# Early products of the first layer: two matmuls of 256 columns into one sum, in place of one of 512 columns

## The chip, the cores and the metric

The kernel runs on one NeuronCore of a Trainium2 chip. The time is what the device takes for one execution, in microseconds. The kernel before took 904.02 us in the median of three runs (903.44 to 906.75).

## The reference

A graph of 3125 nodes with 256 features and 103125 edges, sorted by destination. `x` is normalised and passed through a relu, then three graph convolutions follow, are added to `x`, are normalised again, and one message-passing step with a GRU cell ends it. Cut to what matters:

```python
deg = segment_sum(ones, dst) ; dinv = rsqrt(deg)          # self-loops included
def conv(h, W, b):                                        # three times
    h = h @ W
    return segment_sum(h[src] * (dinv[src] * dinv[dst]), dst) + b
h = relu(layernorm(x))
x = x + conv(relu(conv(relu(conv(h, W1, b1)), W2, b2)), W3, b3)
h = relu(layernorm(x))
red = segment_sum(h[src] + relvectors[edge_type], dst)
x = x + gru_cell(red, h)
```

The kernel replaces gather and segment sum by products with a dense matrix of edge counts, `count` (source nodes by destination nodes, small integers in f16). The factors `dinv` go to the rows of the table before the product and to the rows of the sum behind it. So that f16 suffices, each table of node rows is held as two f16 parts: a high part, and a low part with what the high one leaves over.

## The kernel before

Nodes lie in T = 25 tiles of 128 (the last has 53). `count` is `[128, 25, CW]`: tile of sources, then column of the destination. `node_a` and `node_b` are `[128, 25, 2, 256]`: tile, part (0 high, 1 low), feature.

**Building `count`** (`build_pe`, `build_dve`, `build_act`, `build_sp`, lines 797 to 1232). The edges go through in NS = 202 steps of 512. For each step VectorE writes one-hot rows (`one_hot`, line 927; for two steps at a time, into three sets of buffers), TensorE makes four matmuls of 175 columns (line 815) into a window of 20 destinations in one of four PSUM banks, with one of 25 columns (line 826) for edges that pass into the next window, and ScalarE copies the window into `count` (line 1127). Each fourth step has four matmuls of 80 columns for the relations (line 855). The columns of three of the four matmuls are computed by register instructions of TensorE's sequencer (`span_of`). TensorE waits for the one-hot rows and for the copy of the window three steps before; VectorE waits until TensorE is through with the set of buffers.

**The first layer beside it.** From step 18 on the table of the first layer is ready in `node_a`. Since the edges are sorted, whole columns of `count` are final early, and the first layer's sums for destination tiles 0 to 20 (`EARLY = 21`) are made while `count` is still being built: 21 x 25 = 525 matmuls (`early_product_pe`, line 909), laid between the matmuls of the windows by a fixed schedule (`products_after`, line 753), two or three in a step. The stationary operand is `count[:, t, u * P:u * P + m]`, the moving one the 512 columns of both parts of `node_a` tile `t`; the sums of tile `u` take a whole PSUM bank, one of three (`out_slot`): 256 columns from the high part, 256 from the low. After the last window the tiles 21 to 24 follow in the same manner (line 1287, 100 matmuls).

**Behind each tile.** VectorE takes the sums (`out_bias_dve`, line 1088): line 1094 scales the low half and adds the bias into `scaled`, line 1097 scales the high half and adds `scaled` into `work` and frees the bank. ScalarE applies relu and factor (line 1105) and writes the high part (line 1109), VectorE the low part (line 1114), and SyncE stores the tile to DRAM (line 1187), from which it is read back into `node_b` after the last window. In the order of its instructions VectorE reaches line 1094 about 5 steps after the tile's last product, and line 1114 about 12 steps after it.

**Afterwards** the second and third layer and the message step use `sums_pe` (line 1258: table stationary, `count` moving, 512 columns and a last chunk of 53), `conv_pe` (line 1269, f32) and the GRU (lines 590 to 685, f32).

Of the kernel before, what the change touches and what calls it, by code (L numbers as in the profile page):

```python
# [5 lines left out]
ALU = mybir.AluOpType  # L6
# [5 lines left out]
P = 128  # L12
# [13 lines left out]
REL_BANK, OUT_BANK = 4, 5  # L26
# [4 lines left out]
OUT_SLOTS = 3  # L31
# [20 lines left out]
def program(nc, x, src, dst, rel, convs, relvec, w_ih_t, w_hh_t, b_ih, b_hh, x1_dram, table_dram, out):  # L52
    N, D = x.shape
    E = src.shape[0]
    R = relvec.shape[0]
    T = -(-N // P)
# [19 lines left out]
    SP, PE, DVE, ACTE, POOL = nc.sync, nc.tensor, nc.vector, nc.scalar, nc.gpsimd  # L76

    def rows(t):
        return P if t < T - 1 else TAIL

    with ExitStack() as ctx:
        def sb(name, shape, dt):
            return ctx.enter_context(nc.sbuf_tensor(name, shape, dt))

        def sem(name):
            return ctx.enter_context(nc.semaphore(name))


        count = sb("count", [P, T, CW], F16)
        node_a = sb("node_a", [P, T, 2, D], F16)  # L90
# [5 lines left out]
        work = [sb(f"work{i}", [P, D], F32) for i in range(2)]  # L96
        scaled = [sb(f"scaled{i}", [P, D], F32) for i in range(2)]
        xt = [sb(f"xt{i}", [P, D], F32) for i in range(2)]
# [9 lines left out]
        newt = sb("newt", [P, 4, T], F32)  # L108
# [6 lines left out]
        ps = ctx.enter_context(nc.psum_tensor("ps", [P, 8, BANK], F32))  # L115
# [137 lines left out]
        dve_seq, act_seq = Count(sem("dve_seq")), Count(sem("act_seq"))  # L253
# [72 lines left out]
        def settled(u):  # L326

            return SETTLE_FIRST + SETTLE_STEP * (u // 2) + SETTLE_ODD * (u % 2)
# [427 lines left out]
        summed_at = [next(s for s in range(NS) if products_after[s] >= (u + 1) * T) for u in range(EARLY)]  # L756

        def out_slot(u):

            return ps[:, OUT_BANK + u % OUT_SLOTS, :]  # L760

        def turned_x(t):
            return h1[:, t, :].rearrange("p (f n) -> p f n", f=HALVES)
# [33 lines left out]
        def build_pe():  # L797
            PE.wait_ge(keys_out, 5)
            offset_words.extend(load_offsets(1))
            for s in range(NS):  # L800
# [42 lines left out]
                for u, t in due[len(between):]:  # L843
                    early_product_pe(u, t)

        def between_pe(products, j):
            for u, t in products[len(products) * j // (QUARTERS - 1):len(products) * (j + 1) // (QUARTERS - 1)]:
                early_product_pe(u, t)
# [60 lines left out]
        def early_product_pe(u, t):  # L909
            m = rows(u)  # L910
            if t == 0:
                PE.wait_ge(win_written, settled(u))
                PE.wait_ge(tile_looped, u + 1)
                if u >= OUT_SLOTS:
                    PE.wait_ge(conv_read, u - OUT_SLOTS + 1)
                else:
                    PE.wait_ge(table_ready, T)
            last = PE.matmul(out_slot(u)[0:m, :], count[:, t, u * P:u * P + m], node_a[:, t, :, :].rearrange("p a d -> p (a d)"),  # L918
                             start=(t == 0), stop=(t == T - 1), skip_group_check=True)
            if t == T - 1:  # L920
                last.then_inc(conv_done, 1)

# [18 lines left out]
        def build_dve():  # L941
# [26 lines left out]
            for u in range(EARLY):  # L968
                if summed_at[u] + OUT_AT >= NS:
                    out_bias_dve(u)  # L970
                if summed_at[u] + OUT_LOW_AT >= NS:
                    out_low_dve(u)
# [115 lines left out]
        def out_bias_dve(u):  # L1088
            m, k = rows(u), u % 2
            DVE.wait_ge(conv_done, u + 1)  # L1090
            DVE.wait_ge(bias1_in, 16)
            if u >= 2:
                DVE.wait_ge(node_scaled, u - 1)
            DVE.scalar_tensor_tensor(out=scaled[k][0:m, :], in0=out_slot(u)[0:m, D:2 * D], scalar=newt[0:m, 1, u:u + 1], in1=xt[1][0:m, :],
                                     op0=ALU.mult, op1=ALU.add).then_inc(*dve_seq.up())
            DVE.wait_ge(*dve_seq.now)
            DVE.scalar_tensor_tensor(out=work[k][0:m, :], in0=out_slot(u)[0:m, 0:D], scalar=newt[0:m, 1, u:u + 1], in1=scaled[k][0:m, :],
                                     op0=ALU.mult, op1=ALU.add).then_inc(conv_read, 1)

        def out_shape_act(u):  # L1100
# [143 lines left out]
        def sums_pe(h, nodes, c, f, tail_rows, ready_at, between):  # L1244

            cols = min(CHUNK, N - c * CHUNK)
            b, read = sums_bank(h)
            if read:
                PE.wait_ge(sums_out, read)
            first = ready_at is not None  # L1250
            sources = [t for t in order if t != T - 1] if first else range(T - 1)

            for n, t in enumerate([T - 1, *sources] if h % 2 and tail_rows == TAIL else [*sources, T - 1]):
                k = P if t < T - 1 else tail_rows
                if first:
                    PE.wait_ge(*ready_at(t))
                for part in range(2):
                    last = PE.matmul(ps[:, b, 0:cols], nodes[0:k, t, part, f * P:(f + 1) * P],  # L1258
                                     count[0:k, t, c * CHUNK:c * CHUNK + cols],
                                     start=(n == 0 and part == 0), stop=(n == T - 1 and part == 1))  # L1260
                if n == T - 1:
                    last.then_inc(sums_done, 1)
                between(n)
# [15 lines left out]
        def layers_pe():  # L1279

            PE.wait_ge(win_written, NS)
            PE.wait_ge(chunk_looped, 1)
            for u in range(EARLY, T):
                m = rows(u)
                PE.wait_ge(conv_read, u - OUT_SLOTS + 1)
                for t in range(T):
                    last = PE.matmul(out_slot(u)[0:m, :], count[:, t, u * P:u * P + m], node_a[:, t, :, :].rearrange("p a d -> p (a d)"),  # L1287
                                     start=(t == 0), stop=(t == T - 1))
                last.then_inc(conv_done, 1)

            for layer, nodes in ((1, node_b), (2, node_a)):
                h0 = (layer - 1) * H_LAYER
                for i, c in enumerate(chunks):
                    for f in range(HALVES):
                        ready_at = None if i or f else first_ready if layer == 1 else (lambda t: (node_ready, T + place[t] + 1))
                        sums_pe(h0 + HALVES * i + f, nodes, c, f, TAIL, ready_at, nothing)
                        if f == 0 and i:
                            convs_pe(layer, h0, i - 1)
                convs_pe(layer, h0, NC - 1)

            h0 = 2 * H_LAYER
            PE.wait_ge(chunk_looped, 2)
            PE.wait_ge(rel_placed, NS)
            due = []
            for i, c in enumerate(chunks):
                for f in range(HALVES):
                    def between(n):
                        if n == T // 2 and due:
                            gru_pe(h0, due.pop(0))
                    sums_pe(h0 + HALVES * i + f, node_b, c, f, REL_ROW + R, (lambda t: (node_ready, 2 * T + place[t] + 1)) if i == 0 and f == 0 else None, between)  # L1310
                    if due:
                        gru_pe(h0, due.pop(0))
                assert not due
                due = [place[t] for t in tiles_of[c]]
            for n in due:
                gru_pe(h0, n)

        def convs_pe(layer, h0, i):
            c = chunks[i]
            PE.wait_ge(sums_out, h0 + HALVES * (i + 1))  # L1320
            PE.wait_ge(w_in[layer], 16)
            for t in tiles_of[c]:
                conv_pe(layer * T + place[t], layer, t, t * P - c * CHUNK, agg)
# [3 lines left out]
        def gru_pe(h0, n):  # L1327
            t = order[n]
            i = chunks.index(t * P // CHUNK)
            at_col = t * P - chunks[i] * CHUNK  # L1330
            PE.wait_ge(sums_out, h0 + HALVES * (i + 1))
            gru_tile_pe(order, n, [gru_sums[i % 2][f][:, at_col:at_col + rows(t)] for f in range(HALVES)])
# [222 lines left out]
        with nc.If(verdict_reg == 0):  # L1555
            build_pe()
            layers_pe()
            build_dve()
            layers_dve()
            build_act()  # L1560
            layers_act()
            build_sp()
            layers_sp()
            fast_pool()
# [174 lines left out]
        with nc.Else():  # L1739
            for t in range(T):  # L1740
# [7 lines left out]
                                     op0=ALU.mult, op1=ALU.mult).then_inc(*dve_seq.up())  # L1748
# [92 lines left out]
```

## Time and profile before

| | |
|---|---|
| median of three runs | 904.02 us (903.44 to 906.75) |
| the profiled execution, whole | 906.02 us |
| its span in the profile | 902.1 us |
| granted TensorE clock, mean over the span | 0.988 |
| build of `count` with early products | 97 to 288 us of the span |
| products of tiles 21 to 24 | 288.6 to 310.4 us |

The page gives for each engine its busy time; a matmul's recorded length contains the time in which it runs out of the array, so that lengths of neighbours overlap, and the distance from one start to the next is what a matmul costs TensorE. Idle time is counted only where nothing recorded runs, so waits shorter than that overlap are seen in the starts alone. `x4` in a row of the timeline means four instructions merged: the length reaches from the first one's start to the last one's end.

### The profile page before, as it was taken

To read this page: it belongs to the slowest core of one execution; us is meant where nothing else is said; L and a number is where in the kernel's file an instruction comes from. 1 tells how busy PE (TensorE), PEld (TensorE's weight loads), DVE (VectorE), ACT (ScalarE), POOL (GpSimd) and SP (SyncE) were. 2 spreads that over 40 slices of the span, in tenths; PEclk is the share of its full clock that TensorE was granted. 3 is DMA by queue.
4 is the path that set the end of the run, shared out by engine and by line. 5 is a ranking of instruction groups with operands and counts; after the bars stand their busy time and mean duration, and the time that the engine had idled before them with its cause. 6 is when DMAs were issued, how large, how long until landed. Compare 5 with 4: busy or idle time off the path is not lost.

```text
span 902.1 us, 14157 instructions
## 1 busy us (share of the span) xinstructions
PE 862.2 (96%) x4870; PEld 480.5 (53%) x4870; DVE 451.5 (50%) x1139; ACT 290.3 (32%) x609; POOL 82.0 (9%) x244
## 2 busy tenths in 40 slices
PE   2689999999999999999999999999999999999996
PEld 1348666666666454444455444445464555555554
DVE  6966899999996211221041433227162233333336
ACT  3365667667675100110020201222231112222122
POOL 0210300111000055540000000000000000000000
PEclk9989999999999999999999999999999999999999
DMA  6100000000001400000000101112310000000001
GB/s 197 31 2 1 3 17 22 17 16 23 16 23 50 137 3 3 3 2 1 1 0 30 47 23 41 38 39 70 123 33 20 12 24 24 24 24 24 24 26 42
DMA packets 36998, 28.34 MB, mean 31 GB/s; under 512 B 12869, under 2 KB 35553, under 8 KB 36924
## 3 DMA queue, kind: packets, MB, share of 16 engines
q1 hardware_dynamic: 36252, 26.97, 9.9%
q8 instruction: 43, 0.70, 0.3%
q10 hardware_dynamic: 672, 0.41, 0.2%
q14 instruction: 31, 0.25, 0.1%
HBM read 17.56 MB, written 9.81 MB: 30 GB/s over the span
## 4 chain that ended last, share of the span: by engine, by line
PE 92%; DVE 4%; ACT 1%; issue 1%; SPq 0%; DMA 0%; DVEq 0%
PE ps L1258 43%; PE ps L918 13%; PE ps L815 8%; PE ps L1269 5%; PE ps L640 5%; PE ps L643 5%; PE ps L1287 2%; PE ps L648 2%; PE ps L651 2%; PE ps L899 2%; PE ps L867 1%; DVE node_b L927 1%; PE ps L855 1%; PE ps L887 1%; PE ps L627 1%
## 5 line engine op out<-in xcount | busy, mean ns | idle before, releaser
L1258 PE MATMUL ps<-count,node_b 128*128 128x512 f16 (+3 forms) x1400 | 270.5, 351 | 0.4 <-DVE node_b L1419 0.3
L1258 PEld LDWEIGHTS ps<-count,node_b 128*128 128x128 f16 (+2 forms) x1400 | 121.5, 97 | 142.3 <-issue 7.6
L918 PE MATMUL ps<-node_a,count 128*128 128x512 f16 x525 | 180.4, 381 | 0.2 <-DVE node_a L1041 0.2
L815 PE MATMUL ps<-node_b 128*128 128x175 f16 x808 | 163.6, 257 | 12.0 <-issue 7.8
L927 DVE TENSOR_TENSOR node_b<-node_b 128x1024 f16<-128x1024 f16 (+2 forms) x253 | 157.4, 671 | 0.0
L1127 ACT ACTIVATE count<-ps 128x500 f32 x202 | 123.0, 609 | 72.9 <-PE ps L815 68.5
L1258 PE MATMUL ps<-count,node_a 128*128 128x512 f16 (+2 forms) x700 | 134.7, 352 | 0.0
L815 PEld LDWEIGHTS ps<-node_b 128*128 128x128 f16 x808 | 79.9, 100 | 41.1 <-issue 11.5
L1258 PEld LDWEIGHTS ps<-count,node_a 128*128 128x128 f16 (+1 forms) x700 | 60.0, 97 | 73.9 <-issue 7.1
L1349 DVE SCALAR_TENSOR_TENSOR work<-ps,dinv,params 128x256 f32<-128x256 f32 (+1 forms) x25 | 12.0, 481 | 124.3 <-PE ps L1269 124.3
L667 DVE TENSOR_TENSOR node_a<-ps,node_a 128x512 f32<-128x512 f32 (+1 forms) x25 | 17.2, 690 | 94.1 <-PE ps L643 94.1
L918 PEld LDWEIGHTS ps<-node_a,count 128*128 128x128 f16 x525 | 53.2, 101 | 18.7 <-ACT count L1127 0.4
L1428 ACT ACTIVATE agg<-ps,scales 128x512 f32<-128x512 f32 (+1 forms) x36 | 22.8, 639 | 120.2 <-PE ps L1258 120.2
L1551 POOL TENSOR_TENSOR count<-count,node_a 16x20 f16 x202 | 45.0, 223 | 90.6 <-DMA chapter_starts<-in_dst 49.0
L1399 DVE SCALAR_TENSOR_TENSOR work<-ps,dinv,params 128x256 f32<-128x256 f32 (+1 forms) x25 | 12.1, 484 | 79.3 <-PE ps L1269 78.6
L604 ACT ACTIVATE node_a<-ps 128x256 f32<-128x256 f32 (+1 forms) x25 | 9.5, 380 | 122.1 <-PE ps L627 122.1
L1269 PE MATMUL ps<-params,agg 128*128 128x256 f32 (+1 forms) x200 | 46.8, 386 | 1.6 <-ACT agg L1428 1.6
L643 PE MATMUL ps<-node_a 128*128 128x512 f32 (+1 forms) x100 | 47.0, 592 | 0.0
L1269 PEld LDWEIGHTS ps<-params,agg 128*128 128x128 f32 (+1 forms) x200 | 36.3, 187 | 11.6 <-issue 4.2
L934 POOL TENSOR_TENSOR count<-count,ident 128x128 f16<-128x128 f16 x21 | 25.2, 1201 | 156.9 <-ACT count L1127 156.9
L826 PE MATMUL ps<-node_b 128*128 128x25 f16 x201 | 39.1, 194 | 0.0
L1424 ACT ACTIVATE node_a<-scaled 128x256 f16<-128x256 f32 (+1 forms) x25 | 10.4, 418 | 78.7 <-DVE scaled L1359 78.7
(211 smaller groups left out, 805.3 us busy)
## 6 DMA issues: line engine op xcount, KB each, us to landing
node_a<-in_x SPq DMA_DIRECT2D x4, 768.0 KB, 8.4
table_scratch<-agg SPq DMA_DIRECT2D x21, 128.0 KB, 1.8
node_b<-table_scratch SPq DMA_DIRECT2D x3, 768.0 KB, 6.5
xt<-x_scratch SPq DMA_DIRECT2D x16, 128.0 KB, 2.2
out<-scaled SPq DMA_DIRECT2D x16, 128.0 KB, 1.7
xt<-in_x SPq DMA_DIRECT2D x12, 128.0 KB, 2.0
params<-in_x SPq DMA_DIRECT2D x12, 128.0 KB, 2.1
x_scratch<-xt SPq DMA_DIRECT2D x12, 128.0 KB, 1.7
```

The lines of the kernel that those rows point to most:

```text
L640: PE.matmul(ps[0:m, rz, 0:2 * D], sums[f], w_ih_sb[:, f, 0:2 * D], start=(f == 0), stop=False)
L643: done = PE.matmul(ps[0:m, rz, 0:2 * D], hs[f], w_hh_sb[:, f, 0:2 * D], start=False, stop=(f == HALVES - 1))
L815: return PE.matmul(window(s)[:, :, keys], low, key_hot[k][:, j, :, i].rearrange("p (t w) -> p t w", w=SPAN), start=(s == 0 and j == 0), st ...
L826: PE.matmul(window(s + 1)[:, :, 0], low, carry_hot[s // GROUP % 2][:, s % GROUP // 2, :, i], start=True, stop=False, skip_group_check=True)
L918: last = PE.matmul(out_slot(u)[0:m, :], count[:, t, u * P:u * P + m], node_a[:, t, :, :].rearrange("p a d -> p (a d)"), start=(t == 0), st ...
L927: return DVE.tensor_tensor(to, iota, keys.unsqueeze(2).to_broadcast([P, n, width, 2]), ALU.is_equal)
L934: done = engine.tensor_tensor(diagonal, diagonal, ident16[:, :].unsqueeze(1).to_broadcast([P, full - first, P]), op)
L1127: ACTE.activation(to, window(s), ACT.Copy).then_inc(win_written, 1)
L1258: last = PE.matmul(ps[:, b, 0:cols], nodes[0:k, t, part, f * P:(f + 1) * P], count[0:k, t, c * CHUNK:c * CHUNK + cols], start=(n == 0 and ...
L1269: done = PE.matmul(ps[0:m, b, 0:D], sums[:, f, at_col:at_col + m], weight[i % 2][:, f, :], start=(f == 0), stop=(f == HALVES - 1))
L1428: ACTE.activation(to[:, 0:cols], ps[:, sums_bank(h)[0], 0:cols], ACT.Copy, scale=inverse_scale).then_inc(sums_out, 1)
L1551: POOL.tensor_tensor(to, to, chapter_counts[chapter % 2][:, at_place // GROUP, at_place % GROUP, :], ALU.add).then_inc(rel_placed, 1)
```

## The change

The sums of a tile take 256 columns of the bank in place of 512. Where there was one matmul with the 512 columns of both parts as moving operand, there are two with 256 columns each, the high part's and the low part's, with the same stationary operand `count[:, t, ...]`, both adding into the same 256 columns. The first of the 50 matmuls of a tile starts the sum and the last ends it. VectorE's two instructions on the sums become one: scale the sum and add the bias. The order of the products among the window matmuls, the number of early tiles, the three banks and all waits are as before.

```diff
         def out_slot(u):
-
-            return ps[:, OUT_BANK + u % OUT_SLOTS, :]
+            return ps[:, OUT_BANK + u % OUT_SLOTS, 0:D]
...
-            last = PE.matmul(out_slot(u)[0:m, :], count[:, t, u * P:u * P + m], node_a[:, t, :, :].rearrange("p a d -> p (a d)"),
-                             start=(t == 0), stop=(t == T - 1), skip_group_check=True)
+            for part in range(2):
+                last = PE.matmul(out_slot(u)[0:m, :], count[:, t, u * P:u * P + m], node_a[:, t, part, :],
+                                 start=(t == 0 and part == 0), stop=(t == T - 1 and part == 1), skip_group_check=True)
             if t == T - 1:
                 last.then_inc(conv_done, 1)
...
-            DVE.scalar_tensor_tensor(out=scaled[k][0:m, :], in0=out_slot(u)[0:m, D:2 * D], scalar=newt[0:m, 1, u:u + 1], in1=xt[1][0:m, :],
-                                     op0=ALU.mult, op1=ALU.add).then_inc(*dve_seq.up())
-            DVE.wait_ge(*dve_seq.now)
-            DVE.scalar_tensor_tensor(out=work[k][0:m, :], in0=out_slot(u)[0:m, 0:D], scalar=newt[0:m, 1, u:u + 1], in1=scaled[k][0:m, :],
+            DVE.scalar_tensor_tensor(out=work[k][0:m, :], in0=out_slot(u)[0:m, :], scalar=newt[0:m, 1, u:u + 1], in1=xt[1][0:m, :],
                                      op0=ALU.mult, op1=ALU.add).then_inc(conv_read, 1)
...
                 for t in range(T):
-                    last = PE.matmul(out_slot(u)[0:m, :], count[:, t, u * P:u * P + m], node_a[:, t, :, :].rearrange("p a d -> p (a d)"),
-                                     start=(t == 0), stop=(t == T - 1))
+                    for part in range(2):
+                        last = PE.matmul(out_slot(u)[0:m, :], count[:, t, u * P:u * P + m], node_a[:, t, part, :],
+                                         start=(t == 0 and part == 0), stop=(t == T - 1 and part == 1))
                 last.then_inc(conv_done, 1)
```

## Rows read from the trace of the kernel before

**Rows 1.** The page: busy time, and tenths busy in forty slices of the span.

```profile
PE 862.2 (96%) x4870; PEld 480.5 (53%) x4870; DVE 451.5 (50%) x1139; ACT 290.3 (32%) x609; POOL 82.0 (9%) x244
...
PE   2689999999999999999999999999999999999996
...
PEclk9989999999999999999999999999999999999999
```

**Rows 2.** The page: the chain that ended last, by line, shares of the span.

```profile
PE ps L1258 43%; PE ps L918 13%; PE ps L815 8%; PE ps L1269 5%; PE ps L640 5%; PE ps L643 5%; PE ps L1287 2%; PE ps L648 2%; PE ps L651 2%; PE ps L899 2%; PE ps L867 1%; DVE node_b L927 1%; PE ps L855 1%; PE ps L887 1%; PE ps L627 1%
```

**Rows 3.** Groups by line, 150 to 270 us: busy us, mean ns, idle before.

```profile
L918 PE MATMUL ps<-node_a,count 128*128 128x512 f16 x327 | 113.5, 381 | 0.0
L815 PE MATMUL ps<-node_b 128*128 128x175 f16 x469 | 95.1, 254 | 0.0
L927 DVE TENSOR_TENSOR node_b<-node_b 128x1024 f16<-128x1024 f16 (+2 forms) x146 | 91.2, 673 | 0.0
...
L826 PE MATMUL ps<-node_b 128*128 128x25 f16 x117 | 22.5, 193 | 0.0
...
L855 PE MATMUL ps<-params 128*80 128x80 f16 x116 | 9.4, 206 | 0.0
```

**Rows 4.** Busy us from 150 to 270: all, PE, PEld, DVE, ACT, POOL.

```profile
150.00:270.00 120.00, 120.00 (x1029) 81.32 (x1027) 118.25 (x244) 84.10 (x173) 13.95 (x14) 1.00 0.07 19
```

**Rows 5.** Waits from 97 to 311 us: us in total, times, longest.

```profile
DVE params L927 <- PE ps L815: 1.9, 6, 0.5
...
PE ps L918 <- DVE node_a L1041: 0.2, 1, 0.2
```

**Rows 6.** Matmuls in order of time: start us, us, line.

```profile
202.07 0.38 PE L918 MATMUL ps<-node_a,count 128*128 128x512 f16 x1
202.29 0.25 PE L815 MATMUL ps<-node_b 128*128 128x175 f16 x1
...
202.68 0.19 PE L826 MATMUL ps<-node_b 128*128 128x25 f16 x1
202.71 0.38 PE L918 MATMUL ps<-node_a,count 128*128 128x512 f16 x1
202.92 0.43 PE L815 MATMUL ps<-node_b 128*128 128x175 f16 x3
```

**Rows 7.** Weight loads of the same stretch, in order of time.

```profile
202.07 0.10 PEld L815 LDWEIGHTS ps<-node_b 128*128 128x128 f16 x1
202.29 0.10 PEld L918 LDWEIGHTS ps<-node_a,count 128*128 128x128 f16 x1
```

**Rows 8.** Matmuls in order of time: the products after the last window.

```profile
288.64 21.86 PE L1287 MATMUL ps<-node_a,count 128*128 128x512 f16 x100
```

**Rows 9.** Matmuls of 53 columns, each with its own weight load.

```profile
337.64 0.84 PE L1258 MATMUL ps<-count,node_b 128*128 128x53 f16 x27
```

**Rows 10.** Two f32 matmuls of 128 columns, and f32 ones of 256 before them.

```profile
887.95 1.03 PE L648 MATMUL ps<-node_a 128*128 128x256 f32 x4
...
889.67 0.38 PE L627 MATMUL ps<-ident,scaled 128*128 128x128 f32 x2
889.89 1.45 PE L640 MATMUL ps<-node_a,agg 128*128 128x512 f32 x3
```

**Rows 11.** VectorE in order of time, around one finished tile.

```profile
199.89 0.48 DVE L1094 SCALAR_TENSOR_TENSOR scaled<-ps,newt,xt 128x256 f32<-128x256 f32 x1
200.40 0.48 DVE L1097 SCALAR_TENSOR_TENSOR work<-ps,newt,scaled 128x256 f32<-128x256 f32 x1
200.80 0.32 DVE L927 TENSOR_TENSOR params<-node_b 128x320 f16<-128x320 f16 x1
...
206.26 0.33 DVE L927 TENSOR_TENSOR params<-node_b 128x320 f16<-128x320 f16 x1 [0.35 <-PE ps L815]
```

**Rows 12.** Line 815, instructions of TensorE's sequencer: ns min, median, max.

```profile
L815 PEldq FUSED_REGOPS  x606: 99/218/245, 26.5 to 285.1; - x152
```

**Rows 13.** VectorE in order of time: the end of this layer's last tile.

```profile
312.55 0.42 DVE L1114 TENSOR_TENSOR node_b<-agg,node_b 53x256 f16<-53x256 f32 x1 [0.70 <-ACT node_b L1109]
```

## The prediction, made before the changed kernel had run

> **What bounds the kernel now.** I read the page first. Over the whole span TensorE (PE) is busy 96%, VectorE 50% [rows 1], and the chain that ended last is almost wholly TensorE's [rows 2]: line 918, the early products, has 13% of the span there, line 815, the windows, 8%, and line 1287, the last four tiles, 2%. The granted clock is at nine tenths or more from the fourth slice on [rows 1] and 1.00 from 150 to 270 us [rows 4], so no change of clock is at stake where the change acts (97 to 310 us).
>
> The share of the whole span hides what matters here: in the stage that the change touches, VectorE is nearly as full as TensorE. From 150 to 270 us both read as full, TensorE 120.00 and VectorE 118.25 of 120 us [rows 4]. So the first question is which of the two sets the pace, since the change gives work to one and takes it from the other.
>
> The listed waits answer it in one direction only: from 97 to 311 us VectorE waited six times for TensorE's line 815, 1.9 us together, and TensorE's matmuls waited once for VectorE, 0.2 us at the first product [rows 5]. But a matmul's recorded length overlaps the next one's, so a short wait of TensorE can't be seen as idle time. I therefore counted its starts. A matmul of 512 columns costs 0.217 us: in the run of 100 after the last window it is (21.86 - 0.38) / 99 [rows 8], and among the windows the next start follows after 0.21 to 0.22 us as well [rows 6]. A window matmul of 175 columns costs 0.088 us, (0.43 - 0.254) / 2 from the three merged ones, and the one of 25 columns 0.03 us [rows 6]. The relations' ones of 80 columns are put at their share of the columns, 80 / 512 x 0.217 = 0.034. With the counts of 150 to 270 us [rows 3] that is 327 x 0.217 + 469 x 0.088 + 117 x 0.03 + 116 x 0.034 = 71.0 + 41.3 + 3.5 + 3.9 = 119.7 of 120 us. TensorE goes from matmul to matmul without a hole; it sets the pace, and VectorE follows with about 0.35 us to spare for each tile (the wait at 206.26 [rows 11]).
>
> **The change part by part.**
>
> *Columns.* 512 columns stream for each product before and after. No gain and no loss.
>
> *One more matmul and one more weight load for each product*, 525 beside the windows and 100 after them, 625 in all, all on the path that sets the end. What a matmul of 256 f16 columns with a full weight load costs isn't in the trace, so it is bounded. Nearest below: matmuls of 53 columns, each with its own load of 128 columns, follow each other at (0.84 - 0.19) / 26 = 0.025 us [rows 9] (0.19 being the length of a short one [rows 3]). A straight line from there to 512 columns at 0.217 gives 256 columns 0.110 us. Nearest by the work: an f32 matmul of 256 columns costs (1.03 - 0.38) / 3 = 0.217 us, as much as 512 in f16, so an f32 one of 128 columns stands for 256 in f16; two of them start at 889.67 and end with the next line's start at 889.89, 0.110 us each [rows 10]. Both say that two halves cost 0.220 us where one product cost 0.217: +3 ns. The low end is 0 (twice 256 columns can't be less than their share of 0.217). The high end is the row in the same stage that costs most above its columns: line 815 takes 0.088 us where 175 columns have a share of 0.074, 14 ns above; at 14 ns for each half on top of 0.1085 a product would cost 0.245, +28 ns. I take +3 ns, since both nearest rows agree on it and line 815 differs from a product in more than its length (it writes runs of 7 columns scattered over the window, at a column computed in a register). Sum: 625 x 3 ns = 1.9 us. Ends: 0, and 525 x 28 + 100 x 3 ns = 15 us.
>
> The weight load itself is hidden: it starts together with the matmul before it (both at 202.07, again at 202.29) and is recorded with 0.10 us [rows 6, 7], within the 0.110 us of a half; and rows 9 show loads that go by at 0.025 us.
>
> Of a matmul's cost the Trainium skill says otherwise, in "TensorE: Matmul & The Clock Gate", section "Back-to-back issue gap": in a stream of pairs of weight load and matmul it gives 81 ns for 128 columns and 131 ns for 512. By a line between these figures, an estimate from that page, 256 columns would cost 98 ns and a product in two halves 65 ns more than one, 41 us over 625. This trace does not bear it out: 512 columns cost 0.217 us in pairs [rows 8]. The page's other formula there, for a single matmul, comes to the same +2.5 ns as the rows.
>
> *VectorE.* The second of the two instructions on a tile's sums goes, with the wait between them. Now they take from 199.89 to 200.80 us, 0.91; one alone takes from 200.40 to 200.80, 0.40 [rows 11]. So 0.51 us for each of 25 tiles, 12.7 us of VectorE's time. Beside the windows it is worth nothing as long as TensorE has no hole: VectorE comes to its limit of three sets of one-hot buffers earlier and waits there for line 815. After the windows nobody waits for it: the last tile's low part ends at 312.97 us [rows 13], while the second layer, which begins when the run of rows 8 is through, near 310.4, uses that tile as its 25th source, 48 matmuls or 10.4 us later. This cover is 8 us wide; gone, each tile would still be served sooner than before.
>
> *The bank.* It is free 0.51 us earlier; with three banks and about nine steps for a tile TensorE never waits for it (no such wait in rows 5). ScalarE gets its input earlier, too, and waits less after the windows; it isn't late anywhere.
>
> *TensorE's sequencer.* It must hand over 1250 instructions more. In a step it has three groups of register instructions of about 0.22 us [rows 12], 0.65 us, and some 9 pairs of load and matmul (1029 matmuls in 120 us [rows 4], a step being 120 x 4 / 469 = 1.02 us). Pairs are handed over at 0.025 us or faster [rows 9]. After the change there are 11.6 pairs, at most 0.29 us: together 0.94 of about 1.03 us. It fits, with 0.09 us to spare for its semaphore waits. Cost: nothing from the rows.
>
> Sum: span 902.1 + 1.9 = 904.0 us, the profiled execution 906.02 + 1.9 = 907.9. It was 2.0 us above the median of the runs, so for the median 904.02 + 1.9 = 905.9 us. That is +0.2%; a measurement of this kernel tells about 0.5% (4.5 us) from no change, so I forecast "no difference".
>
> **The rivals.**
>
> *Short matmuls cost more than their columns (slower).* Place: the 525 products beside the windows. Mechanism: what makes line 815 cost 14 ns above its columns belongs to every matmul issued between windows, not to its scattered output. For it: also the 25 columns there take 0.03 us. Against it: in the same place 512 columns cost no more than after the windows (0.21 to 0.22 [rows 6]). Price: 525 x 28 + 100 x 3 ns = 15 us, 919 us. It decides from 4.5 us / 625 = 7 ns for each product on.
>
> *The load isn't hidden, or the sequencer runs dry (slower).* If the second load of the same weights came on top, at rows 9's 25 ns, 625 x 25 ns = 16 us, 920 us; at its recorded 0.10 us [rows 7] 63 us, 967 us. This is also what the page's pair figures would amount to. If handing over a pair took more than 0.025 + 0.09 / 11.6 = 0.033 us, the sequencer would set the pace; at 0.04 us a step would take 1.11, 0.08 more in each of some 184 steps, 15 us. Against both: rows 7 and 9.
>
> *VectorE sets the pace (faster).* For it: 118.25 of 120 us busy [rows 4]. Then 21 tiles x 0.51 = 10.7 us would go: 893 us. Against it: the sum of starts that fills 119.7 of 120 us, and that it is VectorE that waits. A small form of this, a few holes that my rounded durations hide (0.3 of 120 us), is worth under 0.5 us.
>
> That the change doesn't do what it says is hardly possible: the instruction of VectorE is gone from the program.
>
> **How the numbers follow.** The forecast (0 to 7 ns for a product) has 0.85 and its own range is 903.0 to 908.5 us: 0 to 4.4 us more, and 1 us down for holes and for the scatter of a median (the runs before spread from 903.44 to 906.75). Short matmuls at a higher price 0.08, of which the lower half would stay below 912. Load or sequencer 0.04. VectorE 0.03. The range for 8 times in 10: 903.0 to 910.0 us. It takes in +9 ns for a product and leaves out the far ends that only a rival reaches. Faster by over 0.5% (below 899.5) 0.03; within 0.5% 0.85; slower (above 908.5) 0.12.
>
> **What would show it.** In the new trace from 97 to 311 us: 1250 matmuls of 256 columns at lines 918 and 1287; in the run after the last window 200 of them in (22.0 + 0.3) us, that is 0.110 us from start to start; the second layer begins near 312.3 us and everything behind it is shifted by the same 1.9 us. VectorE's busy time falls from 451.5 to about 440 us, and its wait for line 815 in this stage grows from 1.9 us to about 10. TensorE's starts still leave no hole. Wrong it would be if the run after the last window shows more than 0.112 us a matmul (the price of the short matmul), if that run is right but the stage from 97 to 288 us has grown by more than 4 us (holes, then the sequencer or the windows), or if that stage has become shorter (VectorE had set the pace).

## The result, and the profile after

The changed kernel took 907.07 us in the median of 12 runs (904.96 to 908.25), the kernel before, in 12 runs beside it, 905.53 us (903.44 to 906.75). The ratio is 1.0018, with a 95% interval of 1.0011 to 1.0025: 1.5 to 1.6 us slower, a difference that is measured and is below the half per cent called "no difference". The profiled execution went from 906.02 to 907.76 us, its span from 902.1 to 903.7.

The page of the changed kernel, answering to [rows 1] and [rows 2]. TensorE has 625 matmuls and as many weight loads more; VectorE is busy 10.0 us less.

```profile
PE 863.4 (96%) x5495; PEld 541.1 (60%) x5495; DVE 441.5 (49%) x1114; ACT 290.0 (32%) x609; POOL 74.8 (8%) x244
...
PE   2689999999999999999999999999999999999996
...
PEclk9989999999999999999999999999999999999999
...
PE ps L1255 43%; PE ps L918 13%; PE ps L814 8%; PE ps L1266 5%; PE ps L640 5%; PE ps L643 5%; PE ps L1285 2%; PE ps L648 2%; PE ps L651 2%; PE ps L898 2%; PE ps L866 1%; DVE node_b L927 1%; PE ps L854 1%; PE ps L886 1%; PE ps L627 1%
```

The groups by line from 150 to 270 us (busy us, mean ns, idle before), answering to [rows 3], and the busy times of the same stretch (all, PE, PEld, DVE, ACT, POOL), answering to [rows 4]. Line numbers below the change are a little lower: 814 and 825 are the 815 and 826 of before.

```profile
L918 PE MATMUL ps<-node_a,count 128*128 128x256 f16 x649 | 113.5, 273 | 0.0
L814 PE MATMUL ps<-node_b 128*128 128x175 f16 x466 | 94.6, 254 | 0.0
```

```profile
150.00:270.00 120.00, 120.00 (x1347) 112.37 (x1345) 112.99 (x231) 83.56 (x172) 7.95 (x14) 1.00 0.07 19
```

VectorE fell from 118.25 to 112.99 us there; TensorE reads as full as before. The waits from 97 to 313 us (total, times, longest) say who took up the room, answering to [rows 5]:

```profile
DVE params L927 <- PE ps L814: 10.8, 34, 0.5
```

VectorE's wait for TensorE grew from 1.9 to 10.8 us, that of TensorE for VectorE is the same 0.2 us at the first product. What a matmul costs is in the starts. Matmuls in order of time, answering to [rows 6], and weight loads, to [rows 7]:

```profile
201.32 0.39 PE L918 MATMUL ps<-node_a,count 128*128 128x256 f16 x2
201.54 0.26 PE L814 MATMUL ps<-node_b 128*128 128x175 f16 x1
```

```profile
201.54 0.20 PEld L918 LDWEIGHTS ps<-node_a,count 128*128 128x128 f16 x2
201.75 0.10 PEld L814 LDWEIGHTS ps<-node_b 128*128 128x128 f16 x1
```

The two halves that start at 201.32 are through at 201.54, 0.22 us, as one product was. Their loads fit in: two in 0.20 us. The run after the last window, answering to [rows 8], gives the cost without windows between:

```profile
289.73 22.11 PE L1285 MATMUL ps<-node_a,count 128*128 128x256 f16 x200
311.77 9.46 PE L1255 MATMUL ps<-count,node_b 128*128 128x512 f16 x43
```

(22.11 - 0.27) / 199 = 0.1097 us for a half, 0.2195 for a product against 0.2170: +2.5 ns. The same price shows beside the windows. The first and the last start of line 918, before and after:

```profile
L918 PE MATMUL ps<-node_a,count x525: 376/382/388, 97.1 to 288.4; 128*128 128x512 f16 x175
```

```profile
L918 PE MATMUL ps<-node_a,count x1050: 269/272/282, 97.0 to 289.6; 128*128 128x256 f16 x175
```

From first to last product it is 288.4 - 97.1 = 191.3 us before and 289.6 - 97.0 = 192.6 after: 1.3 us for 525 products, 2.5 ns each. With 0.25 us of the last hundred that is the 1.6 us by which the span grew. This length, from the first to the last start of line 918 (917 or 919 in some kernels), is "the stage" below: 191.3 us before. It holds 184 steps of the build. VectorE around a finished tile, answering to [rows 11], and at the last tile, to [rows 13]:

```profile
200.33 0.47 DVE L1094 SCALAR_TENSOR_TENSOR work<-ps,newt,xt 128x256 f32<-128x256 f32 x1
200.72 0.31 DVE L927 TENSOR_TENSOR params<-node_b 128x320 f16<-128x320 f16 x1
...
202.66 0.32 DVE L927 TENSOR_TENSOR params<-node_b 128x320 f16<-128x320 f16 x1 [0.22 <-PE ps L814]
```

```profile
313.38 0.42 DVE L1111 TENSOR_TENSOR node_b<-agg,node_b 53x256 f16<-53x256 f32 x1 [0.69 <-ACT node_b L1106]
```

One instruction for 0.39 us in place of two for 0.91; 2 us later VectorE stands and waits for a window. The last tile's low part is ready at 313.80 us; the second layer, which starts at 311.77, uses it 10.4 us after that, so it still has 8 us to spare.

### The profile page after: what moved, and what is told of

Same layout as the page of the kernel before. It is cut to its first block, busy times and chain, and to the rows that moved or that the text cites. A ratio compares the mean times of both kernels' runs of the same rounds, so it can differ in the third digit from the quotient of the medians.

```text
span 903.7 us, 15382 instructions
## 1 busy us (share of the span) xinstructions
PE 863.4 (96%) x5495; PEld 541.1 (60%) x5495; DVE 441.5 (49%) x1114; ACT 290.0 (32%) x609; POOL 74.8 (8%) x244
## 4 chain that ended last, share of the span: by engine, by line
PE 92%; DVE 4%; ACT 1%; issue 1%; DMA 0%; SPq 0%; DVEq 0%
PE ps L1255 43%; PE ps L918 13%; PE ps L814 8%; PE ps L1266 5%; PE ps L640 5%; PE ps L643 5%; PE ps L1285 2%; PE ps L648 2%; PE ps L651 2%; PE ps L898 2%; PE ps L866 1%; DVE node_b L927 1%; PE ps L854 1%; PE ps L886 1%; PE ps L627 1%
## 5 line engine op out<-in xcount | busy, mean ns | idle before, releaser
L918 PE MATMUL ps<-node_a,count 128*128 128x256 f16 x1050 | 181.7, 273 | 0.2 <-DVE node_a L1041 0.2
L918 PEld LDWEIGHTS ps<-node_a,count 128*128 128x128 f16 x1050 | 88.6, 101 | 2.3 <-ACT count L1124 0.4
L927 DVE TENSOR_TENSOR params<-node_b 128x320 f16<-128x320 f16 x101 | 33.1, 328 | 11.1 <-PE ps L814 10.8
L1422 ACT ACTIVATE node_a<-scaled 128x256 f16<-128x256 f32 (+1 forms) x25 | 10.4, 416 | 78.8 <-DVE scaled L1357 78.8
```

The lines of the kernel that those rows point to most:

```text
L927: return DVE.tensor_tensor(to, iota, keys.unsqueeze(2).to_broadcast([P, n, width, 2]), ALU.is_equal)
```

## The experiments

The theory: TensorE's array, fed without a hole, sets the length of the stage; a product costs 2.4 ns more for each matmul that it is cut into; VectorE's relief is worth nothing. Twelve kernels were run. Ratios are to the kernel before, timed on the same chip. Stage and last hundred are read from one profiled execution of each. Many of these kernels do not make the reference's sums: e1 leaves the low part out of the first layer, e6, e7 and e11 leave it out of the products beside the windows, e8 pairs other columns, and e10 to e12 put the counts at other places. They serve for the time alone.

| kernel | ratio (95%) | stage, us | last hundred products, us |
|---|---|---|---|
| before | 1 | 191.3 | 21.86 |
| changed | 1.0018 (1.0011 to 1.0025) | 192.6 | 22.11 |
| e1, one product, one sum instruction | 1.0007 (0.9998 to 1.0016) | 191.2 | 21.86 |
| e2, two halves, two sum instructions | 1.0020 (1.0011 to 1.0029) | 192.6 | 22.11 |
| e3, four of 128 columns | 1.0045 (1.0031 to 1.0059) | 195.3 | 22.61 |
| e4, sums scattered, runs 16 apart | 1.0018 (1.0009 to 1.0027) | 192.6 | 22.11 |
| e5, eight of 64 columns | 1.0308 (1.0291 to 1.0325) | 210.7 | 28.3 |
| e6, high part alone, one sum instruction | 0.9910 (0.9892 to 0.9928) | 181.1 | 22.11 |
| e7, high part alone, two sum instructions | 0.9920 (0.9900 to 0.9940) | 183.1 | 22.11 |
| e8, moving operand with step 2 | 1.0088 (1.0071 to 1.0105) | 197.8 | 22.94 |
| e9, sums scattered, runs 15 apart | 1.0198 (1.0181 to 1.0215) | 206.6 | 24.78 |
| e10, as e5, fixed columns | 1.0120 (1.0103 to 1.0137) | 202.2 | 28.0 |
| e11, as e6, fixed columns | 0.9742 (0.9726 to 0.9758) | 172.9 | 22.11 |
| e12, changed, fixed columns | 0.9974 (0.9964 to 0.9984) | 194.2 | 22.11 |

### e1: VectorE's part alone

```diff
-            DVE.scalar_tensor_tensor(out=scaled[k][0:m, :], in0=out_slot(u)[0:m, D:2 * D], scalar=newt[0:m, 1, u:u + 1], in1=xt[1][0:m, :],
-                                     op0=ALU.mult, op1=ALU.add).then_inc(*dve_seq.up())
-            DVE.wait_ge(*dve_seq.now)
-            DVE.scalar_tensor_tensor(out=work[k][0:m, :], in0=out_slot(u)[0:m, 0:D], scalar=newt[0:m, 1, u:u + 1], in1=scaled[k][0:m, :],
+            DVE.scalar_tensor_tensor(out=work[k][0:m, :], in0=out_slot(u)[0:m, 0:D], scalar=newt[0:m, 1, u:u + 1], in1=xt[1][0:m, :],
```

> The kernel before with VectorE's part of the change alone: line 1094 (scale of the low half) is left out, line 1097 adds the bias; the product stays one matmul of 512 columns. The low part of the first layer's table is so left out of the sum. Theory (TensorE sets the pace): no difference, 0 us within 0.7, ratio 1.000; VectorE is busy about 12 us less and waits for line 815 about 9 us more. Rival (VectorE sets the pace): 21 x 0.51 = 10.7 us less, ratio 0.988.

Measured: no difference (1.0007, the interval holds 1), and the stage has its old length. The relief went into waiting, here from 97 to 311 us:

```profile
DVE params L927 <- PE ps L815: 9.9, 34, 0.5
```

1.9 us have become 9.9. These 8.0 us are not the whole of 21 x 0.51 = 10.7: VectorE's recorded lengths overlap as well (0.48 us long, with the next start after 0.40 [rows 11]), and waits shorter than the overlap are not listed. VectorE does not set the pace, although it was busy 118 of 120 us.

### e2: the changed matmuls with VectorE's old load

```diff
+            DVE.scalar_tensor_tensor(out=scaled[k][0:m, :], in0=out_slot(u)[0:m, :], scalar=newt[0:m, 1, u:u + 1], in1=xt[1][0:m, :],
+                                     op0=ALU.mult, op1=ALU.add).then_inc(*dve_seq.up())
+            DVE.wait_ge(*dve_seq.now)
             DVE.scalar_tensor_tensor(out=work[k][0:m, :], in0=out_slot(u)[0:m, :], scalar=newt[0:m, 1, u:u + 1], in1=xt[1][0:m, :],
```

> The changed kernel with VectorE's load put back: its instruction on the sums runs twice, first into a buffer that nobody reads, with the wait between. Theory: as the changed kernel, 1.3 to 1.9 us above the kernel before (ratio 1.0018), since TensorE alone pays. Rival (the two halves of the change cancel: the products cost more and VectorE's relief gives it back): clearly above the changed kernel, by up to 10 us, ratio up to 1.013.

Measured: 1.0020, as the changed kernel's 1.0018. So no gain of VectorE's hides a larger price of the matmuls; with e1 the change is taken apart: TensorE's part is the whole of it.

### e3 and e5: more and shorter matmuls

```diff
             for part in range(2):
-                last = PE.matmul(out_slot(u)[0:m, :], count[:, t, u * P:u * P + m], node_a[:, t, part, :],
+                for at_col in range(0, D, 128):
+                    last = PE.matmul(out_slot(u)[0:m, at_col:at_col + 128], count[:, t, u * P:u * P + m], node_a[:, t, part, at_col:at_col + 128],
```

(e5: 64 in place of 128; the 100 products after the last window in the same way.)

> The changed kernel with four matmuls of 128 columns for each product. From 0.217 us for 512 columns and 0.1097 for 256 a matmul costs 2.4 ns and 0.419 ns for each column; 128 columns then 0.056, a product 0.224, +7 ns over the kernel before, 625 x 7 = 4.5 us, ratio 1.005. Rival (the load of 0.10 us shows once the matmul is shorter than it): at least 4 x 0.1 = 0.4 us for a product, over 110 us more, ratio over 1.12. Rival (TensorE's sequencer sets the pace): the run after the last window still shows 0.056, but the stage beside the windows grows by more than 4 us.

> The changed kernel with eight matmuls of 64 columns for each product, 4375 matmuls and as many loads more than before. By 2.4 ns and 0.417 ns for each column a matmul costs 0.029, a product 0.233, +17 ns over the kernel before, 10 us, ratio 1.011 to 1.012. Rival (TensorE's sequencer sets the pace once it hands over some 28 pairs in a step beside its register instructions): the run after the last window shows 0.029 for each, but the stage beside the windows grows by much more than 9 us.

e3 came as worked out: 1.0045, and the run after the last window shows the price:

```profile
290.49 22.61 PE L1287 MATMUL ps<-node_a,count 128*128 128x128 f16 x400
```

(22.61 - 0.22) / 399 = 0.0561 us. A matmul of 128 columns goes by in less time than its load is recorded with (0.10 us), and no load shows: the rival with the load falls.

e5 missed my number. The stage grew by 19.4 us, not by the 9 that 525 x 17 ns make, and the run after the last window by 6.4 us, not by 1.7. In that run, in order of time, a hole stands:

```profile
308.37 7.36 PE L1287 MATMUL ps<-node_a,count 128*128 128x64 f16 x243
318.59 18.05 PE L1287 MATMUL ps<-node_a,count 128*128 128x64 f16 x557 [2.86 <-issue]
```

The first 243 keep to the price, (7.36 - 0.19) / 242 = 0.0296 us; 2.9 us are then lost in one place, put down to "issue": TensorE had nothing to run, and no wait on another engine is named. The rest go at 0.032 on average. The rival with TensorE's sequencer held for the stage; e10 tests it.

### e4 and e9: the sums scattered over the bank

(The matmuls and VectorE's instruction address the sums in the same runs; those lines are left out here.)

```diff
-            return ps[:, OUT_BANK + u % OUT_SLOTS, 0:D]
+            return ps[:, OUT_BANK + u % OUT_SLOTS, :].rearrange("p (a w) -> p a w", w=16)[:, :, 0:8]      # e4
+            return ps[:, OUT_BANK + u % OUT_SLOTS, 0:480].rearrange("p (a w) -> p a w", w=15)[:, :, 0:8]  # e9
```

> The changed kernel with the 256 sums of a product written as 32 runs of 8 columns, 16 columns apart, in the same bank (VectorE reads them there). Line 815 costs 12 to 14 ns above its columns and writes 25 runs of 7. If the runs are the cause: 0.4 to 0.55 ns a run, 13 to 18 ns a half, 26 to 36 ns a product, 16 to 22 us more than the changed kernel, ratio 1.02 to 1.026. Rival (it is its place between others, or the column from a register): no difference to the changed kernel, ratio 1.002.

> As the kernel with the scattered sum, but the 32 runs of 8 columns lie 15 columns apart in place of 16, so that most begin off a boundary of 8 columns, as line 815's runs of 7 at steps of 20 do. Of the 10 ns that line 815 costs above 2.4 ns and its columns, the step of two in its moving operand explains 4 (a half with step 2 took 0.1139 in place of 0.1097). If the boundaries are the rest, a half costs 0.115 here, 625 x 11 ns = 7 us more than the changed kernel, ratio 1.009. Rival: no cost, ratio 1.002.

e4 cost nothing: 0.1097 us for a half as before, 192.6 us for the stage. e9, the same number of runs one column closer, cost much more than I had put down. Its run after the last window:

```profile
303.08 24.78 PE L1286 MATMUL ps<-node_a,count 128*128 128x256 f16 x200
```

(24.78 - 0.29) / 199 = 0.1231 us, 13.4 ns above e4's half, and with 14.0 us more in the stage the largest effect of all the kernels that keep the number of matmuls. So it isn't that sums are scattered but how the runs lie: on average 0.42 ns for each of 32 runs. Where they begin and how far apart they lie were changed together, and not taken apart: at 15 apart 28 of the 32 runs begin off a multiple of 8 columns, 16 of them at an odd column, and the gap between them is 7 columns in place of 8.

### e6 and e7: TensorE relieved

```diff
-            for part in range(2):
-                last = PE.matmul(out_slot(u)[0:m, :], count[:, t, u * P:u * P + m], node_a[:, t, part, :],
-                                 start=(t == 0 and part == 0), stop=(t == T - 1 and part == 1), skip_group_check=True)
+            last = PE.matmul(out_slot(u)[0:m, :], count[:, t, u * P:u * P + m], node_a[:, t, 0, :],
+                             start=(t == 0), stop=(t == T - 1), skip_group_check=True)
```

(e7 has besides e2's second instruction of VectorE.)

> The changed kernel, in which the early products beside the windows (not the 100 after them) leave the low part out: one matmul of 256 columns each, TensorE's load there falls by 525 x 0.109 = 57 us. Theory: VectorE sets the pace next. It had 1.9 us of waits in the kernel before and is relieved of 21 x 0.51 us: the stage from 97 to 288 us becomes 12 to 13 us shorter and no more, ratio 0.986. Rival (VectorE has more room than its busy time says, because its lengths overlap): up to 57 us shorter, ratio 0.94.

> As the one before it, but VectorE's instruction on the sums runs twice, as in the kernel before the change. Theory: with TensorE out of the way VectorE's relief has its full price: this is 21 x 0.51 = 10.7 us longer than the one before it, ratio 0.998 to the kernel before. Rival (something else sets the pace there, TensorE's sequencer or ScalarE): the difference between the two is under 5 us.

57 us of TensorE's work are gone, and the stage of e6 is 11.5 us shorter than the changed kernel's, 10.2 shorter than before: near the 12 to 13 that I expected, but for another reason. (The ratio, 0.9910, missed the 0.986 that I had put down.) e7 is only 2.0 us longer than e6 in the stage, not 10.7, so VectorE did not set e6's pace. The waits say what did. First the kernel before, from 97 to 311 us, then e6 and e7, from 97 to 300 us:

```profile
PEld ps L815 <- issue: 0.4, 2, 0.2
```

```profile
PEld ps L814 <- issue: 37.8, 190, 0.4
...
DVE params L926 <- PE ps L814: 2.0, 9, 0.3
```

```profile
PEld ps L814 <- issue: 38.7, 200, 0.3
...
PEld ps L814 <- DVE node_b L926: 3.3, 10, 0.9
```

In e6 the weight load of a window matmul stood 190 times for "issue", 37.8 us together, where before there were two such waits: I read this as the sequencer not having handed it over, and e11 tests it. VectorE's 118.11 of 120 us busy in e6 was again no sign of the bound. In e7 the waits for VectorE appear beside those for issue, and the chain that ended last goes through VectorE for 21% of the span, in e6 for 4%; the two are nearly level there:

```profile
PE 74%; DVE 21%; issue 2%; ACT 2%; SPq 0%; DMA 0%; DVEq 0%; ACTq 0%
```

### e10, e11, e12: without register instructions

```diff
-            if j == 0:
-                return slice(0, SPAN)
+            if j < QUARTERS:
+                return slice((0, 5, 10, 13)[j], (0, 5, 10, 13)[j] + SPAN)
```

(on e5 for e10, on e6 for e11, on the changed kernel for e12)

> The kernel with eight matmuls of 64 columns, with the columns of the window matmuls fixed at 0, 5, 10 and 13, so that TensorE's sequencer has no register instructions (the counts then stand at other places than the reference's). Theory (register instructions and many pairs together overload the sequencer): the step goes from 1.127 to the array's 1.07, 184 steps, 10 us shorter, ratio 1.020; the run after the last window stays at 0.035 a matmul. Rival (the handing over of the matmuls alone sets the pace): as with register instructions, ratio 1.031.

> The kernel with the high part only and one instruction of VectorE on the sums, with the same fixed columns (places of the counts are other ones again). Its step was 0.974. Theory (TensorE's sequencer with its register instructions set that pace): without them VectorE is next; at two instructions a tile it held 0.985, at one it can do 0.985 - 0.51 / 9 = 0.928, so 184 x 0.046 = 8.5 us less, ratio 0.982. Rival (VectorE or ScalarE set it already): no change, ratio 0.991.

> The changed kernel with the same fixed columns. Theory (TensorE's array sets the pace and the column from a register costs it nothing): as the changed kernel, ratio 1.002, step 1.032. Rival (the register instructions are what holds the step, or what line 815 costs above its columns): 606 x 10 ns = 6 us or more shorter, ratio 0.995 or below.

e11: the stage falls from 181.1 to 172.9 us, 8.2 us, where 8.5 were expected for VectorE as the next bound, and TensorE now waits for VectorE (97 to 270 us):

```profile
PEld ps L814 <- DVE node_b L926: 37.4, 81, 0.8
...
PE ps L814 <- DVE node_b L926: 14.3, 35, 0.5
```

The waits for "issue" at line 814 are down from 37.8 us to 0.6. So e6's pace was the sequencer's with its three groups of register instructions. (The ratio fell further, to 0.9742 for an expected 0.982, since the steps before the first product got shorter too: it starts at 91.2 us in place of 96.5.) That 8.2 came so near 8.5 is in part luck: e11 has one hole of 3.2 us at a product (line 917, put down to "issue"), and VectorE's one-hot instructions were longer there than in e6, 705 ns for 671 (line 926, its larger forms, 150 to 270 us). Its 172.9 us is what VectorE did in this kernel, not VectorE's limit.

e10: the stage falls from 210.7 to 202.2 us, which is the changed kernel's 192.6, six more matmuls at 2.4 ns for each of 525 products, 7.6 us, and 2.0 us left over, of which the fixed columns alone bring 1.6 (e12 below). The run after the last window, where no register instruction was before, kept its 28 us. Both are near what was expected, and the register instructions cost 8.5 us of e5's stage: eight pairs for a product together with them overload the sequencer. (The ratio came out at 1.0120 and not 1.020, as the first product starts 4.8 us earlier here, too.)

e12: by the ratio, 0.9974, neither side was right; the stage decides. First and last start of line 918:

```profile
L918 PE MATMUL ps<-node_a,count x1050: 268/273/283, 91.4 to 285.6; 128*128 128x256 f16 x175
```

194.2 us, not shorter than the changed kernel's 192.6. From one start of line 814 to the next matmul it is 87.4 ns on average in place of 85.7 (110 to 260 us of the span); that this comes of the other columns to which the windows go is likely but not shown. The whole kernel still gains, since the first product starts 5.6 us earlier. Within the stage of the changed kernel the register instructions bring no gain when they go, so the sequencer is not its bound. For the price of a single window matmul the kernel before says it more directly: the first of the four in a step has its column fixed at 0, and it takes 88.9 ns to the next start on average, the three with a column from a register 83 to 85.

### e8: the moving operand with a step of two

```diff
-                last = PE.matmul(out_slot(u)[0:m, :], count[:, t, u * P:u * P + m], node_a[:, t, part, :],
+                last = PE.matmul(out_slot(u)[0:m, :], count[:, t, u * P:u * P + m],
+                                 node_a[:, t, :, :].rearrange("p a d -> p (a d)").rearrange("p (d i) -> p d i", i=2)[:, :, part],
```

> The changed kernel with the same 512 columns split otherwise: the first matmul takes the even ones, the second the odd ones, so its moving operand is read with a step of two elements, as line 815's is (the sums are then other ones than the reference's). If the step is what makes line 815 cost 12 to 14 ns above its columns, a half costs 0.120 or more in place of 0.110, 625 x 20 to 30 ns = 12 to 19 us more, ratio 1.015 to 1.022. Rival (it is not the step): as the changed kernel, ratio 1.002.

Between the two: its run after the last window

```profile
294.26 22.94 PE L1285 MATMUL ps<-node_a,count 128*128 128x256 f16 x200
```

gives (22.94 - 0.28) / 199 = 0.1139 us, +4.2 ns a half, and the stage 5.2 us. The step explains a part of what line 815 costs above its columns, no more.

## Why the prediction was right

**The bound.** "TensorE goes from matmul to matmul without a hole; it sets the pace" is shown by e1 and e2: each half of the change was run alone, and only TensorE's changed the time. The sum of starts (119.7 of 120 us) had read this rightly where the busy shares, 120.00 and 118.25, could not. Alone it was no proof: the window matmul's 0.088 us was read in the same stage, so that a short wait in each of them would have been counted as its price. e1 and e12 exclude VectorE and the sequencer as the cause of one.

**The price of the second matmul.** Taken at +3 ns, measured +2.5 ns in both places; the straight line from 53 to 512 columns had given 0.110 us and the trace gives 0.1097. 625 x 2.5 ns = 1.6 us against the forecast 1.9. Doubling the number of matmuls once more (e3) cost 4.1 us against 4.5, so the price goes by the number of matmuls and not by this one split. Of the two rows that the +3 ns stood on only the straight line could carry it (2.8 ns by its own numbers). The f32 pair, 0.22 us read from starts given to 0.01, could have been some ns more or less; that it agreed was partly luck.

**The weight load.** Hidden, as taken; down to 0.056 us a matmul (e3). None of the prices for a load that shows came, neither 16 nor 63 us, nor the 41 us that the pair figures gave (the rival takes them for the same as the 16 or the 63, which they are not).

**VectorE.** 0.52 us saved a tile in place of 0.51, its busy time 441.5 for the forecast 440, its wait for line 815 10.8 for "about 10". Worth nothing in time, as taken. The "0.35 us to spare for each tile" was misread: it is one wait, and the list has six in 21 tiles, 1.9 us, 0.09 a tile. The list of waits in turn says too little: with the array relieved and VectorE's load as before (e7) the stage is 8.2 us shorter, 0.39 us a tile. So the figure came near for a reason that the prediction did not have. I was wrong, too, on what it would be worth if TensorE made room: the price of 10.7 us in the rival assumed that VectorE is next. e6 and e7 differ by 2.0 us: with VectorE's one instruction TensorE's own sequencer is next. Put in order by the stage: TensorE's array 191.3 (192.6 changed), VectorE with two instructions 183.1 (nearly level with the sequencer), the sequencer with its register instructions and one pair a product 181.1, VectorE with one 172.9 or less (e11, with its hole).

**The sequencer.** "It fits" held, but the sum behind it, 0.94 us, was too small. For e6, which hands over 9 pairs in a step, that sum gives 0.65 + 9 x 0.025 = 0.88 us; measured are 181.1 / 184 = 0.98. Its price of a pair was too high: e5 hands over 20 pairs more in a step and takes 210.7 / 184 = 1.145 us, 8 ns for each. By an estimate from these two, which takes the sequencer to set the pace of both, the changed kernel's sequencer needs 0.98 + 2.9 x 0.008 = 1.01 of its 1.05 us, so it has 0.04 to spare and not 0.09, and e3's needs 1.05 of 1.06 us. The two errors partly cancel. The prediction's second rival had it set the pace from 0.033 us a pair on; at eight pairs a product it did so (e5, e10), by the number of pairs and not by their price.

**The rival of costly short matmuls** rested on line 815. At 2.4 ns and 0.419 ns a column it should cost 0.076 us. The 0.088 was read at one place; from 110 to 260 us it is 0.0854 on average, so some 10 ns are its own. The step of two in its moving operand is about 3 of them (e8: 4.2 ns over 256 columns, if it goes by columns). Sums in runs 15 columns apart cost 0.42 ns a run (e9), and line 815 writes 25 runs of 7 at steps of 20 columns; that this is the remainder is only argued, as it isn't known which runs count. A column from a register isn't it, by the first matmul of each step, which has none and costs no less (under e12). None of this applies to a product with contiguous columns, which is why the rival's 15 us never came.

Of the kernels that make the whole sums none is faster than the one before the change.

**The number.** Forecast 905.9 us, measured 907.07; the difference of the two kernels was forecast at 1.9 and is 1.5 between the medians. The 1.2 us that the number is off lie in the base: 904.02 was the median of three runs, 905.53 that of twelve, 1.5 us more, less the 0.3 by which the difference was forecast too high.

## What to carry to other kernels

When two engines both read as full, add up the starts: the one whose starts fill the stretch at costs known from elsewhere probably sets the pace, and a kernel in which only the other is relieved settles it: here its relief turned into waiting. Cutting a matmul in two costs 2.5 ns, down to 128 columns here, as long as the sequencer keeps up; it is a cheap trade against another engine's work, but a trade only where that engine is the bound. Before work is taken off the bound, ask for the next limits, the engine's own sequencer among them.

## What the hardware showed that was not expected

- Sums written in 32 runs of 8 columns cost nothing at a distance of 16 columns and 13.4 ns a matmul at 15 (e4, e9). Whether the starts or the gaps matter is open.
- A moving f16 operand read with a step of two costs 4.2 ns over 256 columns (e8), far from doubling.
- With 29 pairs of load and matmul in a step beside the register instructions the stage is 8.5 us longer than without these (e5, e10); with 17 pairs (e3) the stage is 195.3 us, the 195.2 that its matmuls' price gives. In a dense run of 800 matmuls of 64 columns TensorE stands for "issue", 2.9 us in one hole in e5 and 2.1 in e10. What is late there, the fetching of the instructions or something else, stays open.
- GpSimd's addition of the diagonal (line 934, 14 instructions from 150 to 270 us) took 568 ns in the changed kernel, where VectorE waits often for a window, 996 ns before, 2098 in e7, and 6780 in e11, where VectorE sets the pace. VectorE's instructions are longer in e11, too (above). The profile's lengths on that engine are rough, and the cause wasn't tried. Before, e7, e11:

```profile
L934 POOL TENSOR_TENSOR count<-count,ident 128x128 f16<-128x128 f16 x14 | 13.9, 996 | 107.2 <-ACT count L1127 107.2
```

```profile
L933 POOL TENSOR_TENSOR count<-count,ident 128x128 f16<-128x128 f16 x14 | 29.4, 2098 | 88.0 <-ACT count L1126 88.0
```

```profile
L933 POOL TENSOR_TENSOR count<-count,ident 128x128 f16<-128x128 f16 x13 | 87.9, 6780 | 19.9 <-ACT count L1123 19.9
```
